# Expert visits over lists in halves of 64 rows: rows stationary instead of weights, fewer visits, a shorter slot table

## The chip, the cores and the metric

The kernel runs on one core of one Trainium2 chip. A core has TensorE (PE, matrix products into PSUM), VectorE (DVE), ScalarE (ACT), GpSimd (POOL) and SyncE (SP, which here only issues transfers), and 16 DMA engines that all queues share. The metric is device time in microseconds of one execution. All data is float32.

## The reference, cut to what matters

A vision transformer block on 32 images of 37 tokens (1184 tokens, 256 features): patch embedding, an attention with a gate and no softmax, and a mixture of experts. The change is in the last part:

```python
scores = sigmoid(x @ gate_weight.T)                 # 32 experts, 4 groups
# the best 2 groups, in them the best 6 experts: topidx, weights tw
g = einsum('th,ehi->tei', x, w_gate)                # hidden 128
u = einsum('th,ehi->tei', x, w_up)
eo = einsum('tei,eih->teh', silu(g) * u, w_down)
routed = einsum('te,teh->th', cw, eo)               # 6 experts of each token
lg = topidx[:, 0] // 2                              # one of 16 anchor experts, hidden 64
anchor = ...                                        # the same form, weight 0.1
out = routed + shared + 0.1 * anchor
```

So there are 48 lists of rows: 16 anchor lists with 1184 rows in all, 32 routed lists with 7104 rows in all. How long each list is, is known only when the routing has run.

## The kernel before, in words

**Front, 0 to some 178 us.** Embedding, attention and routing go through six blocks of tokens. For each block DVE computes which row of which list every token takes (`place`, its last instruction is L1245). POOL then scatters the token's row (256 features, the expert weights, the rows of the result) into the list in device memory (`rows_d`) with an indirect DMA per tile and choice, 77 in all (L457). The attention product (`attend`, L618) uses the array in four column strips of 32: 16 matmuls a tile, each strip with its own stationary and its own moving data, written to partitions 32r to 32r+31 of one PSUM bank. Every float32 matmul is two records in the trace, a transpose is one.

**The slot table.** The program is static, the lists are not. So the work is cut into a fixed number of visits of 128 slots, and a table tells for each visit where its rows start, which weights it uses, which column holds its weight and which sum it adds to. DVE computes it from the list lengths in 84 instructions (L1441 to L1524), PE turns the columns into rows (`table_rows`, `slot_bounds`), and DVE copies them to where registers are loaded from (L1530).

**The visits.** There are XT = 112: 25 of kind A (anchors: short lists packed into shared tiles of 128), then 24 of kind F (128 full rows of one expert), 31 of kind X and 32 of kind M (remainders of lists, packed into shared tiles of 128, where one tile can be visited for two or more lists). For visit i

- SP loads a register from the table and issues one load of 128 rows (`load_rows`, L413; six buffers);
- PE turns the rows (two 128x128 transposes, `turn_rows`, L812); ACT or DVE copies them out (L985, L1580);
- ACT copies the up weights of the expert into a buffer (`copy_up`, L981), since a stationary operand can't take its address from a register here;
- PE multiplies with the weights stationary and the turned rows moving (`up`, L823: four matmuls of 128 columns, two for an anchor); the result has the hidden features on partitions;
- ACT takes the silu (L990), DVE the product (`hidden`, L1597), which is already turned as the down product needs it;
- PE multiplies down (`down`, L838: hidden stationary, 256 columns of weights moving, at an address from a register);
- for F, ACT weighs the result and POOL sends it; else DVE adds the weighted rows into the packed tile (`accumulate`, L1589), and POOL sends the tile when its last list has been added (L483, 66 sends in all).

PE's order is written out by hand: `up(i)`, `turn_rows(i + 2)`, `down(i - 1)`. Each engine works its own instructions in order; semaphores join them. POOL issues the sends behind all scatters. At the end SP waits for all sends, loads the seven partial results of every token from `sums_d` (L419), DVE adds them (L1626) and SP stores the output (L434).

Before all this, SP fills 128 rows of zeros ahead of the lists (two DMAs of 7728 KB, L378), and POOL zeroes the packed tiles (L449, L476, L480).

Of the kernel before, what the change touches and what calls it, by code (L numbers as in the profile page):

```python
# [24 lines left out]
P = 128  # L25
# [35 lines left out]
LIST_ROWS = TOKENS  # L61
DUMMY_ROW = P + LISTS * LIST_ROWS
# [7 lines left out]
ROWS_PACKED = -(-TOKENS * TOPK // P)  # L70
LAST_FILLED = TOKENS * TOPK % P
FULL = -(-(TOKENS * TOPK - EXPERTS * (P - 1)) // P)
MIXED = ROWS_PACKED - FULL
EXTRAS = EXPERTS - 1
ANCHOR_PACKED = -(-TOKENS // P)
ANCHOR_TILES = ANCHOR_PACKED + ANCHORS - 1
KINDS = "A" * ANCHOR_TILES + "FFX" * 12 + "XM" * 6 + "XMM" * 13
XT = len(KINDS)
INDEX = [KINDS[:i].count(k) for i, k in enumerate(KINDS)]
TILE_AXIS, EXTRA_AXIS = 1000, 2000  # L80
RING = D + 1
GB = 6
PL = 3 * EXPERTS + ANCHORS


def routed(i):
    return KINDS[i] != "A"


def summed(i):  # L90

    return KINDS[i] != "F"


def sums_before(i):
    return sum(summed(k) for k in range(i))


def copied_by_act(i):
    return KINDS[i] != "F"  # L100


def copies_before(i):
    return sum(copied_by_act(k) == copied_by_act(i) for k in range(i))


def number_of(i):

    return {"A": 0, "F": TILE_AXIS, "M": TILE_AXIS + FULL, "X": EXTRA_AXIS}[KINDS[i]] + INDEX[i]
# [4 lines left out]
TRI4 = 3 * LISTS  # L114
SMALL = TRI4 + 23
PIECES = [[(0, 4), (4, 8), (8, NT)]] * (CHOICES - 1) + [[(0, 4), (4, 7), (7, 9), (9, 10), (10, NT)]]
assert KINDS.count("F") == FULL and KINDS.count("M") == MIXED and KINDS.count("X") == EXTRAS
assert all(KINDS[:i].count("X") >= min(EXTRAS, INDEX[i] + 1) for i in range(XT) if KINDS[i] == "M")
assert FULL * D <= ANCHOR_COLS and XT <= P
LATE_PIECES = 10  # L120
BIG = 3.0e38


def build(nc, pt, wt, posr, brow, wqkv, wo, wg1, wg2, lnwb, gwt, gbias, sgu, sd, wx,
          ident_c, cmask_c, turn_c, parity_c, cs_c, before_c, small_c, out):
    with ExitStack() as ctx:
# [56 lines left out]
        def dense(*shape):  # L183
# [5 lines left out]
            if len(shape) == 2:  # L189
# [13 lines left out]
        until_scattered = cut[0]  # L203
        xrow = dense(NT, ROW)
        padrow = dense(ROW)
        mixed = spent[:, 0:MIXED * RING]
        mixed_rows = mixed.bitcast(I32)
# [5 lines left out]
        of_lists = small[:, 0:3 * LISTS].rearrange("p (q l) -> p q l", q=3)  # L213
        iota_a, base0, tri4 = small[:, LISTS:LISTS + ANCHORS], small[:, 2 * LISTS:3 * LISTS], small[:, TRI4:TRI4 + 16]
        pcol, number, of_number, tile_number, spare_row, last_tile, first_w = (small[:, TRI4 + 16 + q:TRI4 + 17 + q]
                                                                                  for q in range(7))
        ring = sb("ring", [P, ANCHOR_PACKED * RING])
        h = sb("h", [P, NT, D])
        ring_rows = ring[:, :].bitcast(I32)
# [1496 lines left out]
```

## Time and profile before

| what | value |
|---|---|
| runs, us | 420.84, 417.67, 415.27; median 417.67 |
| profiled execution: span, first to last instruction | 412.1 us; the page gives no other time of this execution |
| mean granted TensorE clock | 0.930 |
| busy: PE / DVE / ACT / POOL | 343.3 / 278.0 / 190.0 / 181.7 us |
| chain that ended last, largest shares | PE L823 20%, PE L838 10%, PE L514 6%, PE L812 5% |

The span is what the trace covers; what lies between it and the time of a run is launch and end. A busy share is an average over stages with different limits, so the stages are read one by one in the rows below. In a timeline, a row that ends in x8 stands for eight records in a row; its first number is when the first one started, and the start of the next row tells when the array was free again.

### The profile page before, as it was taken

What the parts mean: (1) busy time and instruction counts of PE and PEld (TensorE: products, weight loads), DVE (VectorE), ACT (ScalarE), POOL (GpSimd) and SP (SyncE); (2) the same over time, 40 slices, a digit from 0 to 9 for tenths busy, and PEclk for the clock granted to TensorE, in tenths of its full rate; (3) what the DMA queues carried; (4) which work ended last, traced back from release to release, by engine and by line L of the source; (5) the groups of instructions that cost most, each with busy time, mean ns of one, the idle gap of its engine ahead of it and who ended that gap; (6) DMA issues with size and microseconds to landing.
All of it is one profiled execution on the core that took longest, in us unless ns stands there. A gap on an engine that the chain in (4) does not pass through costs nothing.

```text
span 412.1 us, 8817 instructions
## 1 busy us (share of the span) xinstructions
PE 343.3 (83%) x2552; PEld 299.1 (73%) x2552; DVE 278.0 (67%) x1171; ACT 190.0 (46%) x471; POOL 181.7 (44%) x159
## 2 busy tenths in 40 slices
PE   5999999999899968773889999999999999994000
PEld 3786978779687857561677789999999999993000
DVE  0466789989798886798357775555565665666675
ACT  1152153441545233400157777777877777771000
POOL 6000000588888768767871374344422344433000
PEclk9999999999999997985989999999999999998555
DMA  7999999986698643694555576555555559531998
GB/s 234 298 335 335 329 341 328 420 320 119 123 337 252 126 96 86 218 387 137 152 162 130 167 214 180 162 158 165 165 145 162 166 155 291 168 113 58 303 303 245
DMA packets 55823, 88.44 MB, mean 215 GB/s; under 512 B 16145, under 2 KB 46521, under 8 KB 55513
## 3 DMA queue, kind: packets, MB, share of 16 engines
q1 hardware_dynamic: 38192, 67.66, 52.9%
q0 software_dynamic: 16720, 19.48, 17.8%
q10 hardware_dynamic: 864, 0.73, 0.6%
q8 instruction: 21, 0.34, 0.3%
q14 instruction: 26, 0.21, 0.2%
HBM read 50.62 MB, written 37.09 MB: 213 GB/s over the span
## 4 chain that ended last, share of the span: by engine, by line
PE 60%; DVE 20%; DMA 8%; issue 3%; ACT 3%; SPq 3%; DVEq 2%; POOLq 0%
PE B L823 20%; PE B L838 10%; PE B L514 6%; PE B L812 5%; DMA W<-sums_d 4%; PE B L549 4%; PE B L632 3%; PE B L598 2%; PE B L618 2%; DVEq L319 2%; DMA e_sb<-rows_d 2%; SPq L419 2%; DVE ring L1589 1%; PE B L656 1%; DMA W<-in_pt 1%
## 5 line engine op out<-in xcount | busy, mean ns | idle before, releaser
L457 POOL DMA_INDIRECT rows_d<-spent,slot x77 | 104.1, 1352 | 97.3 <-issue 90.9
L823 PEld LDWEIGHTS B<-e_sb,UPW 128*128 128x128 f32 x796 | 105.4, 193 | 10.7 <-issue 5.5
L823 PE MATMUL B<-e_sb,UPW 128*128 128x128 f32 x796 | 108.9, 278 | 1.5 <-issue 1.5
L1597 DVE TENSOR_TENSOR e_sb<-e_sb,B 128x128 f32<-128x128 f32 (+1 forms) x112 | 32.3, 288 | 62.2 <-ACT e_sb L990 55.8
L981 ACT COPY UPW<-W 128x512 f32 (+1 forms) x112 | 63.9, 570 | 22.2 <-issue 13.9
L838 PE MATMUL B<-W,e_sb 128*128 x224 | 69.3, 391 | 0.8 <-DVE e_sb L1597 0.8
L483 POOL DMA_INDIRECT sums_d<-spent x32 | 31.1, 972 | 48.7 <-DVE spent L1589 47.9
L812 PE MATMUL B<-ident,e_sb 128*128 128x128 f32 x224 | 43.1, 274 | 1.9 <-DMA e_sb<-rows_d 1.8
L990 ACT ACTIVATE e_sb<-B 128x128 f32<-128x128 f32 (+1 forms) x112 | 30.9, 276 | 22.2 <-PE B L823 20.8
L514 PE MATMUL B<-W 128*111 128x256 f32 (+1 forms) x132 | 34.2, 406 | 4.6 <-DMA W<-in_pt 4.5
L483 POOL DMA_INDIRECT sums_d<-W,tok_full x24 | 23.2, 966 | 30.3 <-ACT W L995 29.7
L838 PEld LDWEIGHTS B<-W,e_sb 128*128 128x128 f32 x224 | 34.0, 192 | 3.5 <-issue 1.7
L985 ACT COPY e_sb<-B 128x256 f32<-128x256 f32 x88 | 32.3, 367 | 4.6 <-PE B L812 4.6
L514 PEld LDWEIGHTS B<-W 128*111 128x111 f32 (+1 forms) x132 | 23.3, 184 | 12.2 <-DMA W<-in_pt 5.3
L1589 DVE SCALAR_TENSOR_TENSOR spent<-B,wcol,spent 128x256 f32<-128x256 f32 (+1 forms) x63 | 30.4, 482 | 1.7 <-DVE spent L1574 0.8
L812 PEld LDWEIGHTS B<-ident,e_sb 128*128 128x128 f32 x224 | 28.5, 144 | 2.3 <-DMA e_sb<-rows_d 2.1
L1626 DVE TENSOR_TENSOR h<-h,W 112x1024 f32<-112x1024 f32 (+3 forms) x23 | 23.2, 1047 | 8.4 <-DMA W<-sums_d 8.4
L1289 DVE TENSOR_TENSOR e_sb<-B,spent 111x444 f32<-111x444 f32 (+1 forms) x44 | 23.6, 597 | 4.1 <-PE B L598 4.1
L1566 DVE TENSOR_TENSOR wcol<-e_sb,turn 128x1 f32<-128x1 f32 x112 | 17.2, 153 | 4.0 <-PE B L812 3.8
L598 PE MATMUL B<-W 32*111 32x222 f32 (+1 forms) x176 | 15.5, 369 | 4.8 <-ACT W L909 4.8
L549 PE MATMUL B<-W 128*128 128x222 f32 (+1 forms) x96 | 18.1, 341 | 0.6 <-ACT W L886 0.6
L606 PE MATMUL B<-spent 128*128 128x256 f32 x70 | 18.6, 414 | 0.0
(250 smaller groups left out, 524.0 us busy)
## 6 DMA issues: line engine op xcount, KB each, us to landing
e_sb<-rows_d SPq DMA_DIRECT2D x112, 161.0 KB, 2.3
rows_d<-spent SPq DMA_DIRECT2D x2, 7728.0 KB, 44.4
W<-in_wx SPq DMA_DIRECT2D x1, 6643.0 KB
W<-sums_d SPq DMA_DIRECT2D x13, 448.0 KB, 9.4
W<-in_wx SPq DMA_DIRECT2D x10, 516.5 KB, 9.5
W<-in_wx SPq DMA_DIRECT2D x1, 4576.0 KB, 18.7
W<-in_pt SPq DMA_DIRECT2D x4, 666.0 KB, 6.9
W<-sums_d SPq DMA_DIRECT2D x7, 336.0 KB, 11.1
```

What stands on the lines that cost most here:

```text
L457: pool.indirect_dma_start(rows_d, bass.IndirectOffsetOnAxis(ap=slot[0:n, t, j:j + 1], axis=0), xrow[0:n, t, :], None).then_inc(done, 16)
L483: pool.indirect_dma_start(sums_d, bass.IndirectOffsetOnAxis(ap=rows, axis=0), src, None).then_inc(done, 16)
L514: m = pe.matmul(B[0][0:TILES[t], i * D:(i + 1) * D], patch_view(b)[:, c, at:at + TILES[t]], w_patch[:, c, :], start=c == 0, stop=c == PC - 1)
L549: m = pe.matmul(B[4 + half][:, c * BT:c * BT + n], w_qkv[:, k, lo:lo + P], xnT[:, k, 0:n], start=k == 0, stop=k == KC - 1)
L812: m = pe.transpose(B[i % 2][:, k * P:(k + 1) * P], G[:, i % GB, k * P:(k + 1) * P], ident[:, :])
L823: mm = pe.matmul(B[2 + i % 2][:, m * P:(m + 1) * P], UPW[:, i % 2, at:at + P], GT[:, i % 2, k, :], start=k == 0, stop=k == KC - 1)
L838: pe.matmul(B[6 + i % 2][:, 0:D], hid[:, i % 2, :], weights, start=True, stop=True).then_inc(D_ps, 1)
L981: act.copy(UPW[:, i % 2, 0:n], W[:, bass.ds(e, size)][:, 0:n]).then_inc(upw_ok, 1)
L985: act.copy(GT[:, i % 2, :, :].rearrange("p k s -> p (k s)"), B[i % 2][:, 0:D]).then_inc(gt_by[True], 1)
L990: act.activation(S[0:n, i % 2, :], B[2 + i % 2][0:n, 0:P], ACT.Silu).then_inc(silu_ok, 1)
L1589: dve.scalar_tensor_tensor(sums, B[6 + i % 2][:, 0:D], wcol[:, i:i + 1], sums, ALU.mult, ALU.add).then_inc(acc_ok, 1)
L1597: dve.tensor_tensor(out[0:n, i % 2, :], S[0:n, i % 2, :], ups, ALU.mult).then_inc(H_ok, 1)
```

## The change

The lists are cut into halves of 64 rows. Each list has its tail of up to 64 rows, and the tails have fixed places: one visit of kind A for each anchor list and one of kind M for each expert, in whose second half (slots 64 to 127) the last 64 rows of that list stand. The weights of a second half are thus known when the program is built; the first half of such a visit takes a full half of any list, at an address from the table. What is left of full rows goes in visits of kind F, 128 rows of one expert (39), and one of kind a. So XT = 88: 16 A, one a, 32 pairs M F, 7 F.

In a visit the rows are now the stationary operand and the weights move, read in place at an address from a register; the copy of the up weights is gone. The result has rows on partitions; so the row's weight is applied in the hidden product, the hidden rows have to be turned by one more transpose and copied, and the down product uses them as stationary rows. Nothing is added up in packed tiles: every visit's result is copied by ACT into a ring of seven buffers and sent by POOL (88 sends), slots without a row to spare rows. The column of a slot's weight is picked by comparing 66 row elements with a code, not by a register. The table needs 22 DVE instructions to its first column; PE loads the weight addresses of four visits at once, SP those of two. The zero fill is 64 rows ahead of each list.

Constants and order:

```diff
-KINDS = "A" * ANCHOR_TILES + "FFX" * 12 + "XM" * 6 + "XMM" * 13
+HALF = P // 2
+LIST_ROWS = TOKENS + HALF
+FULL_GROUPS = (TOKENS * TOPK - TOPK) // HALF
+FULL = -(-(FULL_GROUPS - EXPERTS) // 2)
+KINDS = "A" * ANCHORS + "a" + "MF" * EXPERTS + "F" * (FULL - EXPERTS)
+GB, YB = 8, 7
...
+def pieces(i):
+    return 2 if tailed(i) else 1
...
+def tail_weights(i):
+    return ANCHOR_COLS + INDEX[i] * WX if routed(i) else INDEX[i] * ANCHOR_WX
```

SP and POOL:

```diff
-            for half in range(2):
-                sp.dma_start(of_list[half * P:(half + 1) * P, :, :],
-                             padrow[:, :].unsqueeze(1).to_broadcast([P, LISTS, ROW])).then_inc(empty, 16)
+            sp.dma_start(of_list[0:HALF, :, :],
+                         padrow[0:HALF, :].unsqueeze(1).to_broadcast([HALF, LISTS, ROW])).then_inc(empty, 16)
...
-                row = entry(mybir.EngineType.SP, 1, i, DUMMY_ROW + P)
-                sp.dma_start(G[:, i % GB, :], rows_d[bass.ds(row, P), :]).then_inc(g_ld[i % GB], 16)
+                n = P // pieces(i)
+                for q in range(pieces(i)):
+                    sp.dma_start(G[q * n:(q + 1) * n, i % GB, :], rows_d[bass.ds(rows[q], n), :]).then_inc(g_ld[i % GB], 16)
...
-            pool.memset(spent[:, 0:until_scattered], 0.0).then_inc(mixed_zero, 1)
...
+            for i in range(XT):
+                pool.wait_ge(to_ok, i + 1)
+                pool.wait_ge(Y_ok, i + 1)
+                pool.indirect_dma_start(sums_d, bass.IndirectOffsetOnAxis(ap=to_row[:, i:i + 1], axis=0),
+                                        Y[:, i % YB, :], None).then_inc(sent[i % YB], 16)
```

PE:

```diff
-            stay_busy(12, 3, w_sgu)
+            stay_busy(8, 3, w_sgu)
             table_rows()
             shared_down(3)
-            slot_bounds()
             shared_up(5)
+            table_codes()
...
-            pe.wait_ge(valid_ok, 1)
-            pe.wait_ge(hs_ok, NB - 2)
+            pe.wait_ge(codes_ok, 1)
+            pe.wait_ge(hs_ok, NB)
...
+            def moved(i, q, lo, n):
+                if q == 1:
+                    return W[:, tail_weights(i) + lo:tail_weights(i) + lo + n]
+                size = WX if routed(i) else ANCHOR_WX
+                return W[:, bass.ds(offsets[i], size)][:, lo:lo + n]
...
             def up(i):
...
+                n = 2 * (HIDDEN if routed(i) else ANCHOR_HIDDEN)
+                rows = P // pieces(i)
+                for k in range(KC):
+                    for q in range(pieces(i)):
+                        own = slice(q * rows, (q + 1) * rows)
+                        m = pe.matmul(B[2 + i % 2][own, 0:n], GT[:, i % 2, k, own], moved(i, q, k * n, n),
+                                      start=k == 0, stop=k == KC - 1)
+                m.then_inc(U_ps, 1)
+            def turn_hidden(i):
                 pe.wait_ge(H_ok, i + 1)
+                pe.transpose(B[4 + i % 2][:, 0:P], H[:, i % 2, :], ident[:, :]).then_inc(HT_ps, 1)
+            def down(i):
+                pe.wait_ge(ht_ok, i + 1)
...
+                for q in range(pieces(i)):
+                    own = slice(q * rows, (q + 1) * rows)
+                    m = pe.matmul(B[6 + i % 2][own, 0:D], HT[:, i % 2, own], moved(i, q, lo, D), start=True, stop=True)
+                m.then_inc(D_ps, 1)
...
+            for i in range(XT + 2):
+                if i % PER_LOAD == PER_LOAD - 1 and i + 1 < XT:
+                    load_offsets(i + 1)
+                if i < XT:
+                    up(i)
+                if i >= 2:
+                    down(i - 2)
                 if i + 2 < XT:
                     turn_rows(i + 2)
+                if 1 <= i <= XT:
+                    turn_hidden(i - 1)
```

ACT and DVE:

```diff
-            def copy_up(i):
...
+            def keep_result(i):
                 act.wait_ge(D_ps, i + 1)
+                if i >= YB:
+                    act.wait_ge(sent[i % YB], sent_until(i % YB, i))
+                act.copy(Y[:, i % YB, :], B[6 + i % 2][:, 0:D]).then_inc(Y_ok, 1)
+            def turned_hidden(i):
+                act.wait_ge(HT_ps, i + 1)
...
+                act.copy(HT[:, i % 2, :], B[4 + i % 2][:, 0:P]).then_inc(ht_ok, 1)
+            for i in range(XT + 2):
+                if i < XT:
+                    hidden_silu(i)
+                if i >= 2:
+                    keep_result(i - 2)
+                if 1 <= i <= XT:
+                    turned_hidden(i - 1)
...
+            def pick_columns(i):
+                dve.wait_ge(T_ps, i + 1)
+                dve.scalar_tensor_tensor(picked[:, i % 2, :, :], pick.unsqueeze(1).to_broadcast([P, 2, PICK]), code_of[:, i:i + 1],
+                                         G[:, i % GB, D:ROW].rearrange("p (q e) -> p q e", q=2),
+                                         ALU.is_equal, ALU.mult).then_inc(pick_ok, 1)
+            def sum_columns(i):
+                dve.reduce_sum(meta[:, i, :], picked[:, i % 2, :, :], axis=AX.X).then_inc(meta_ok, 1)
+            def result_rows(i):
+                dve.tensor_tensor(to_row[:, i:i + 1], meta[:, i, 1:2], spare[:, i:i + 1], ALU.add).then_inc(to_ok, 1)
             def hidden(i):
...
+                dve.scalar_tensor_tensor(H[:, i % 2, 0:n], B[2 + i % 2][:, n:2 * n], meta[:, i, 0:1], S[:, i % 2, 0:n],
+                                         ALU.mult, ALU.mult).then_inc(H_ok, 1)
+            for i in range(-2, XT):
+                if i >= 0:
+                    hidden(i)
                 if i + 2 < XT:
+                    pick_columns(i + 2)
+                    turned_copy(i + 2)
+                    sum_columns(i + 2)
+                    result_rows(i + 2)
```

## Rows read from the trace of the kernel before

**Rows 1.** Stages: stretch and its length, then busy us and instructions of each engine.
```profile
core 0: us, PE busy (x) PEld busy (x) DVE busy (x) ACT busy (x) POOL busy (x), PEclk, DMA share, GB/s
178.80:192.60 13.80, 5.49 (x23) 4.39 (x22) 12.81 (x85) 0.00 (x0) 11.05 (x9) 0.75 0.80 272
...
206.50:240.50 34.00, 32.06 (x193) 25.18 (x193) 24.50 (x96) 22.73 (x73) 15.57 (x11) 0.95 0.57 159
240.50:374.00 133.50, 133.50 (x1039) 129.09 (x1039) 78.11 (x348) 102.23 (x259) 55.09 (x58) 1.00 0.57 168
```

**Rows 2.** Timeline of PE in one routed visit: start, length, line, operation, count.
```profile
281.62 0.38 PE L812 MATMUL B<-ident,e_sb 128*128 128x128 f32 x2
281.84 0.60 PE L838 MATMUL B<-W,e_sb 128*128 x2
282.27 1.05 PE L823 MATMUL B<-e_sb,UPW 128*128 128x128 f32 x8
283.16 0.38 PE L812 MATMUL B<-ident,e_sb 128*128 128x128 f32 x2
```

**Rows 3.** Timeline of PE, the up part of two anchor visits in a row.
```profile
226.04 0.65 PE L823 MATMUL B<-e_sb,UPW 128*128 128x128 f32 x4
...
227.32 0.65 PE L823 MATMUL B<-e_sb,UPW 128*128 128x128 f32 x4
```

**Rows 4.** Timeline of PE, attention products in column strips around four transposes.
```profile
36.45 0.98 PE L618 MATMUL B<-e_sb,W 111*32 111x111 f32 x32
37.35 0.60 PE L539 MATMUL B<-ident,W 111*128 111x111 f32 x4
37.88 0.98 PE L618 MATMUL B<-e_sb,W 111*32 111x111 f32 x32
```

**Rows 5.** Timeline of DVE: the last slots, and the end of the table.
```profile
178.63 0.17 DVE L1245 SCALAR_TENSOR_TENSOR slot<-top_slots,ones 111x8 int32<-111x8 f32 x1
...
192.37 0.17 DVE L1524 TENSOR_TENSOR tcol<-tcol 128x1 f32<-128x1 f32 x1
```

**Rows 6.** Timeline of PE: the first rows of the first visit are turned.
```profile
203.14 0.41 PE L812 MATMUL B<-ident,e_sb 128*128 128x128 f32 x2
```

**Rows 7.** SP's row loads: the first six in the timeline; all 112, by line.
```profile
196.85 8.29 SPq L413 DMA_DIRECT2D e_sb<-rows_d  x6
...
DMA to landing us min/median/max: 2.2/2.3/6.2
```

**Rows 8.** POOL's scatters: first of the last tile, last of all; landing of all 77.
```profile
179.11 1.35 POOL L457 DMA_INDIRECT rows_d<-spent,slot  x1 [2.69 <-DVE slot L1245]
...
207.24 1.35 POOL L457 DMA_INDIRECT rows_d<-spent,slot  x1 [0.31 <-issue]
...
DMA to landing us min/median/max: 4.9/8.3/17.8
```

**Rows 9.** POOL's sends: two in a row in the timeline; landing of all 66.
```profile
234.13 0.97 POOL L483 DMA_INDIRECT sums_d<-ring  x1 [0.30 <-DVE ring L1589]
235.41 0.97 POOL L483 DMA_INDIRECT sums_d<-ring  x1 [0.30 <-DVE ring L1589]
...
DMA to landing us min/median/max: 2.4/2.4/4.5
```

**Rows 10.** Groups by line: busy, mean ns; then one instruction of the table, in the timeline.
```profile
L1597 DVE TENSOR_TENSOR e_sb<-e_sb,B 128x128 f32<-128x128 f32 (+1 forms) x112 | 32.3, 288 | 62.2 <-ACT e_sb L990 55.8
L985 ACT COPY e_sb<-B 128x256 f32<-128x256 f32 x88 | 32.3, 367 | 4.6 <-PE B L812 4.6
L1566 DVE TENSOR_TENSOR wcol<-e_sb,turn 128x1 f32<-128x1 f32 x112 | 17.2, 153 | 4.0 <-PE B L812 3.8
L1580 DVE COPY e_sb<-B 128x256 f32<-128x256 f32 x23 | 9.6, 415 | 0.0
187.62 0.33 DVE L1499 SCALAR_TENSOR_TENSOR e_sb<-e_sb,small 128x112 f32<-128x112 f32 x1
```

**Rows 11.** Register loads of SP: ns min/median/max, first and last start.
```profile
L319 SPq TENSOR_LOAD <-scratch x112: 262/268/1447, 195.3 to 363.0; - x112
```

More of the change, by code:

```diff
@@ L212, in build @@
         small = sb("small", [P, SMALL])
[L213 to L217, printed above, removed]
+        (base0, less, carry, cap, list_facts, iota_a, tri4, number, rows_before, from_end, spare_rows,
+         pick) = (small[:, column(name)] for name in COLUMNS)
+        pick_codes = list_facts[:, LISTS:2 * LISTS]
         h = sb("h", [P, NT, D])
-        ring_rows = ring[:, :].bitcast(I32)
         token_row = sb("token_row", [P, 2, NT], I32)
         to_rows = sb("to_rows", [P, NT])
-        spare = sb("spare", [P, 2])
         e_sb = sb("e_sb", [P, 2 * HEADS * TT])
@@ L315, in build, with entries, sent_until @@
         block = ctx.enter_context(nc.Block())
-        def entry(engine, q, i, top):
-            return nc.values_load(table[0:1, q, bass.ds(i, 1)], engines=(engine,), min_val=0, max_val=top,
-                                  skip_runtime_bounds_check_because="the table is computed within these bounds")
+        def entries(engine, of_tiles, top):
+            _, values = nc.values_load_multi_w_load_instructions(
+                of_tiles, engines=(engine,), min_val=0, max_val=top,
+                skip_runtime_bounds_check_because="the table is computed within these bounds")
+            return values
+        def sent_until(k, n):
+            return 16 * len(range(k, n, YB))
         def patch_view(b):
@@ L1413, in _ @@
             place(NB - 1)
-            E = EXPERTS
-            took = [0]
-            def tab(n):
-                v = tabs[:, took[0]:took[0] + n]
-                took[0] += n
-                assert took[0] <= tabs.shape[1]
-                return v
-            starts, ends, total, of_tile, mine = tab(PL), tab(PL), tab(E), tab(E), tab(PL)
-            facts = tab(4 * PL).rearrange("p (q l) -> p q l", q=4)
-            offset, many, shifted, slot_tile = (facts[:, q, :] for q in range(4))
-            held, begin, end, full, lead, behind = tab(LISTS), tab(LISTS), tab(LISTS), tab(E), tab(LISTS), tab(LISTS)
@@ L1428, in _ @@
-            new, away, some, rounded, over, span, own = (tab(LISTS), tab(LISTS), tab(LISTS), tab(E), tab(E), tab(ANCHORS),
-                                                         tab(LISTS))
-            picked = tab(3 * LISTS).rearrange("p (q l) -> p q l", q=3)
-            R, M, X, A = (slice(q * E, q * E + (E if q < 3 else ANCHORS)) for q in range(4))
-            LR, LA = slice(0, E), slice(E, LISTS)
-            ones_of = ones[:, 0:E]
-            def pack(q):
-                return tcol[:, q:q + 1]
```

485 lines of the change are left out of this document (169 added, 316 removed).

## The prediction

> **What bounds the kernel now.** I read the time by stages first. From 240.50 to 374.00 us, the 87 routed visits, TensorE is busy 133.50 of 133.50 us, while DVE has 78.11, ACT 102.23 and POOL 55.09 [rows 1]. That stage is TensorE's alone, so a visit's price is what its records take start to start. The anchor stage before it (206.50 to 240.50) has PE 32.06 of 34.00, yet its visits pace at 1.28 us, 226.04 to 227.32 [rows 3], where their records alone need 0.22 + 0.43 + 4 x 0.111 = 1.09 [rows 2]: there the loop of small steps around PE counts too. Between the routing and the first visit lies the table, 13.80 us with DVE busy 12.81 and PE 5.49 [rows 1].
>
> Second view: TensorE's records inside one routed visit [rows 2]. Two 128-column transposes take 281.62 to 281.84, 0.11 us each; the down matmul, two records of 256 columns, 281.84 to 282.27, 0.215 each; the up part, eight records of 128 columns, 282.27 to 283.16, 0.111 each. Time goes by moved columns, about 0.84 ns per column and record; every matmul is two records, a transpose one. The weight loads hide behind this.
>
> **The main edit: rows stationary, weights moving.** A visit of 128 rows of one expert (F) then has up = 2 matmuls of 256 columns = 4 x 0.215 = 0.86 us, down 0.43, and three transposes instead of two, since the hidden rows must be turned as well: 0.33. Sum **1.62 us**, against 1.54 now (281.62 to 283.16). Per visit this is no gain; the gain is in the number of visits, 88 for 112: 39 F, 32 M, 16 A, one a.
>
> **M and A carry two halves of 64 rows with different weights**, twice as many matmuls, each with 64 stationary columns and its own half of the output partitions. Whether the two halves run side by side decides everything. The kernel has such a case: the attention product (L618), with four column strips of 32. Its 32 records of 111 columns start at 36.45 and the next work starts at 37.35 [rows 4]: 0.90 us, where one after another they would need 32 x 0.093 (111 columns at 0.84 ns) = 2.98. So at least 3.3 of 4 strips overlap, each with its own moving data. I take two halves as fully overlapped. What the tiling costs is its change: 36.45 to 37.88 holds eight waves of L618, four transposes and two changes of tiling; 1.43 - 12 x 0.093 = 0.31 us for two changes. A tailed visit changes twice (into halves before up, out before the transposes). So
>
> - M: 0.86 + 0.43 + 0.33 + 0.31 = **1.93 us**
> - A: up 4 waves x 0.111 = 0.44, + 0.43 + 0.33 + 0.31 = **1.51 us**; a: 1.20 us.
>
> Routed: 39 x 1.62 + 32 x 1.93 = 125.0 us for 133.5, **gain 8.5**. Anchors: now 37.4 us from the first turn at 203.14 [rows 6] to 240.50, of which 25 x 1.28 = 32.0 are pace and 5.4 entry. After: 5.4 + 16 x 1.51 + 1.2 = 30.8, **gain 6.6**. Bounds: changes of tiling cost between nothing (48 x 0.31 = 15 us better) and double (15 worse); half tiles with an address from a register appear in no row.
>
> The Trainium skill speaks against full overlap: "TensorE: Matmul & The Clock Gate", section "Measured speedup vs the span model", has three column tiles at 2.38 times, an estimated 1.6 for two. By it the sum would be some 14 us worse. Our row shows 3.3 of 4 with a change of tiling inside, so the trace agrees with the page only in that a part is lost, and I price that part as the change.
>
> **The table.** 84 DVE instructions, L1441 to L1524, run from 178.83 (right behind L1245 at 178.63) to 192.37 [rows 1, 5], 0.16 us each. The new chain has 22 to its first column, 13 of them waited for: 3.6 us at that mean, 5.5 at 0.25 each, so the column is there at about 184.4, 8 us sooner. The rest then follows as before (10.7 us to the first turn at 203.14), but with other waits. SP issues its first row load at 196.85 [rows 7]; it will still wait for the last tile's anchor scatter, issued at 179.11, which lands after 8.3 us in the median, 17.8 at most [rows 8]. That gives 187.4, a register load of up to 1.4 [rows 11] and a landing of 6.2 [rows 7]: first rows at about 195.5. PE now also waits for all shared adds (hs_ok NB) and for the codes; these shared products and sums already lie inside the 10.7 us, so they keep PE until 195.1 at worst. **Gain 7**, bounds 0 (scatter lands at its latest) to 8.
>
> **What must hide.**
> - *Scatters and sends on POOL.* The last 18 scatters run from 179.11 until 208.59, 1.65 us each, set by the last slots at 178.63; the smaller zero fill frees the first scatter but cannot move this end. All sends queue behind it. ACT's keep_result(7) waits for send 0 (ring of 7), and behind it stand the copy of turned hidden rows and the next silu. Send 0 lands at about 208.6 + 1.0 + 2.4 = 212 [rows 9]; visit 7's result falls at about 195.5 + 5.4 + 9 x 1.5 = 214. Hidden by 2 us. After that POOL needs 1.28 per send (234.13 to 235.41), under every visit but a.
> - *DVE.* Hidden product 0.29, turned copy 0.42, one-column product 0.15 [rows 10]; the picking over 66 elements and its reduction lie between that 0.15 and the 0.33 of the 112-element form, taken 0.25 each. Sum 1.36 by durations, 1.6 with the waits between them: just under F. The register loads leave DVE.
> - *ACT.* Three passes, none above the 0.37 of the 128x256 copy [rows 10]: under 1.1. The weight copies go, but ACT was not the bound.
> - *SP.* M and F together: one register load, 0.27 us (1.4 while scatters run) [rows 11], three row loads of about 0.45 issue; 1.6 us against 3.55. A pair of A visits during scatters: 1.4 + 4 x 0.45 = 3.2 against 3.0, about even, with eight buffers ahead.
> - *PE's register load*, one for four visits instead of one each: no price, PE is gapless with the present ones.
> - Zeroing of packed tiles, fewer row bytes: off the path, nothing.
>
> **Tail.** The same send and reads follow the last down product. Before it stand one more transpose, 0.11 [rows 2], and a copy, 0.37 at most [rows 10], with their hops between engines: **+0.7** (bounds 0.5 and 1).
>
> **Sum.** 8.5 + 6.6 + 7 - 0.7 = 21.4. On the profiled execution: span 412.1 to 390.7. The page gives no time beyond the span; the median of the runs, 417.67, lies 5.6 above, kept: 417.67 - 21.4 = **396 us**.
>
> **The rivals.**
> 1. *The halves do not overlap* (the half whose weights come by register is held on the full array, say): slower than before. Place: up and down of M and A. Price: 32 x (0.86 + 0.43) + 16 x (0.44 + 0.43) = 55 us, time 451. It decides below an overlap r where 55 x (2/r - 1) = 21.4, r = 1.44. For it: every register address in the trace is on a full array. Against: 3.3 of 4 in L618. 0.12.
> 2. *They overlap in part.* Read the 0.90 us as lost overlap, 3.3 of 4 or 0.83 each, and let that come on top of the change: 2 x 0.83 = 1.65, 55 x (2/1.65 - 1) = 12 us, time 408. For it: the strips in our row have another width. 0.10. By the page of the Trainium skill named above it would be 410.
> 3. *Another engine becomes the bound*: DVE's chain, or hidden rows coming late to the turn (PE, copy, down in one visit), at 2.0 us a routed visit: 71 x 2.0 = 142 for 125, time 413. Against: DVE 1.6. 0.07.
> 4. *The table's gain doesn't come* (bound 0, the last anchor scatter landing late): 403. For it: landings up to 17.8. 0.10.
> 5. *The change of tiling costs nothing*, the 0.31 being waits: 381. Against: the records themselves leave 1.12 of the 1.43 us. 0.06.
>
> Forecast 0.55, own range 387 to 402.
>
> **Numbers.** 380 to 411 takes in the forecast, rivals 4 and 5 and most of rival 2: 0.55 + 0.10 + 0.06 + 0.08 = 0.79. 2% of 417.67, about what can be told from no change, is 8.4: faster below 409.3. Faster: forecast, 4, 5 and parts of 2 and 3, 0.71 + 0.05 + 0.02 = 0.78; same: the rest of 2 and 3, 0.10; slower: rival 1, 0.12.
>
> **What would show it.** F visits at 1.6 us and M at 1.9 in TensorE's timeline; in M, pairs of up records starting within some 10 ns, the next pair 0.215 later (0.215 between all records is rival 1); a gap of about 0.15 at each change of tiling; the first turn near 196; PE without idle time from the first M on. Wrong would be: PE waiting on DVE's product or ACT's copy in most visits (rival 3), or the first turn still at 203.

## The result, and the profile after

The changed kernel took **404.37 us** in the median of four executions (403.39 to 404.89), the kernel before 417.65 on the same chip (415.27 to 420.84): ratio **0.966, 95% interval 0.961 to 0.972**, 13.3 us faster. 396 us was forecast; 404.37 lies in the range of 380 to 411. In all that follows, a median takes only executions within 1.5% of the fastest of their kernel, since slower ones count as disturbed.

One correction comes first, as every stage is compared through it. The profiled execution of after took 404.71 us with a span of 402.9, so 1.8 us lie around the span, not 5.6. If as much lay around the span of before (412.1), its profiled execution was one of 413.9 us, 3.8 under the median.

The stages of after: the table, the anchors (first turn to first routed up), the routed visits (to the end of the last up); columns as in [rows 1].

```profile
184.46:189.32 4.86, 3.73 (x11) 2.68 (x9) 4.41 (x23) 0.00 (x0) 3.98 (x3) 0.70 1.04 398
201.23:235.11 33.88, 29.10 (x249) 17.20 (x247) 21.23 (x90) 13.38 (x47) 24.19 (x22) 0.90 0.64 180
235.11:359.45 124.34, 124.34 (x828) 89.13 (x828) 88.33 (x350) 62.68 (x212) 67.69 (x71) 1.00 0.58 174
```

The table is 4.9 us for 13.8, the routed stage 124.3 for 133.5 with PE busy throughout; in the anchors PE is busy 29.1 of 33.9 us only. SP's last wait ahead of the first row load:

```profile
SPq L332 <- DMA rows_d<-spent,slot: 2.6, 1, 2.6
```

It is the wait for a scatter of the last tile, as forecast: SP's first register load starts at 193.24 us, 9.0 behind the last slot (forecast 8.8).

Now PE's timeline through a mixed and a full visit:

```profile
281.24 1.08 PE L838 MATMUL B<-W,e_sb 128*64 x8
282.16 0.60 PE L856 MATMUL B<-W,e_sb 128*64 x4
282.69 0.44 PE L824 MATMUL B<-ident,G 128*128 128x128 f32 x2
282.97 0.27 PE L845 MATMUL B<-ident,e_sb 128*128 128x128 f32 x1
283.07 1.03 PE L838 MATMUL B<-W,e_sb 128*128 x4
283.94 0.59 PE L856 MATMUL B<-W,e_sb 128*128 x2
284.37 0.38 PE L824 MATMUL B<-ident,G 128*128 128x128 f32 x2
284.59 0.27 PE L845 MATMUL B<-ident,e_sb 128*128 128x128 f32 x1
284.79 0.44 PE L838 MATMUL B<-W,e_sb 128*64 x2
```

Start to start, the eight half records of the mixed up take 0.92 us (281.24 to 282.16), the four whole ones 0.87 (283.07 to 283.94): the halves seem to run side by side (experiment 1 asks whether they do). M and F together take 3.55 us (281.24 to 284.79), as forecast (1.93 + 1.62).

Then three lines on the start of the anchors: SP's register loads and row loads (190 to 236 us), ns as minimum/median/maximum, and what PE waited for, in us, times, longest.

```profile
L332 SPq TENSOR_LOAD <-row_table x12: 296/626/1184, 193.2 to 234.4; - x12
L430 SPq DMA_DIRECT2D G<-rows_d x43: 342/469/2146, 194.2 to 235.7; - x43
PE B L824 <- DMA G<-rows_d: 4.1, 5, 1.5
```

The first six register loads, up to 216.3 us, took 0.70 to 1.18 us, the six behind them 0.30 to 0.55. POOL's last scatter starts at 212.9 us, and a scatter lands 4.5 us after its issue at the least.

And the end: the last three sends, VectorE's first adds beside them, and the traffic of the late reads (372 to 391 us).

```profile
361.05 1.07 POOL L498 DMA_INDIRECT sums_d<-e_sb,to_row  x1 [0.45 <-issue]
362.46 1.66 POOL L498 DMA_INDIRECT sums_d<-e_sb,to_row  x1 [0.34 <-issue]
364.43 0.97 POOL L498 DMA_INDIRECT sums_d<-e_sb,to_row  x1 [0.30 <-issue]
...
360.06 3.22 DVE L1525 TENSOR_TENSOR h<-h,W 112x1024 f32<-112x1024 f32 x3
...
DMA packets 1540, 5.06 MB, mean 266 GB/s; under 512 B 193, under 2 KB 193, under 8 KB 1540
```

**The account of the two profiled executions**, 412.1 to 402.9, in us:

| stretch | before | after | forecast | came |
|---|---|---|---|---|
| start to last slot | 178.63 | 184.26 | 0 | +5.6 |
| last slot to first turn | 24.51 | 16.97 | -7 | -7.5 |
| first turn to first routed up | 37.4 | 33.9 | -6.6 | -3.5 |
| to the end of the last up | 133.6 | 124.3 | -8.5 | -9.3 |
| to the first late read | 5.8 | 8.0 | +0.7 | +2.2 |
| late reads to the end | 32.1 | 35.5 | 0 | +3.3 |

Two stages came as forecast. The four others are what experiments 3, 4 and 5 ask about.

### The profile page after: what moved, and what is told of

Read it like the earlier page. It is cut to its first block, busy times and chain, and to the rows that moved or that the text cites. A ratio compares the mean times of both kernels' runs of the same rounds, so it can differ in the third digit from the quotient of the medians.

```text
span 402.9 us, 7999 instructions
## 1 busy us (share of the span) xinstructions
PE 334.5 (83%) x2376; PEld 253.5 (63%) x2376; DVE 275.7 (68%) x1105; ACT 140.9 (35%) x399; POOL 195.0 (48%) x178
## 4 chain that ended last, share of the span: by engine, by line
PE 60%; DVE 14%; DMA 10%; SPq 7%; issue 4%; ACT 3%; POOL 1%; POOLq 0%; DVEq 0%
PE B L838 17%; PE B L856 8%; PE B L514 7%; PE B L824 6%; DMA W<-sums_d 5%; PE B L549 4%; SPq L430 4%; PE B L632 3%; PE B L598 2%; DMA rows_d<-spent,slot 2%; PE B L618 2%; PE B L845 2%; SPq L436 2%; POOL sums_d L498 1%; PE B L656 1%
## 5 line engine op out<-in xcount | busy, mean ns | idle before, releaser
L498 POOL DMA_INDIRECT sums_d<-e_sb,to_row x88 | 85.7, 974 | 65.4 <-ACT e_sb L1010 51.1
L838 PE MATMUL B<-W,e_sb 128*64 (+3 forms) x544 | 87.0, 368 | 0.7 <-DVE e_sb L1495 0.7
L838 PEld LDWEIGHTS B<-W,e_sb 128*64 128x64 f32 (+1 forms) x544 | 50.1, 155 | 15.9 <-issue 9.2
L856 PE MATMUL B<-W,e_sb 128*64 (+2 forms) x272 | 54.0, 389 | 1.2 <-ACT e_sb L1016 1.2
L1510 DVE SCALAR_TENSOR_TENSOR e_sb<-B,meta,e_sb 128x128 f32<-128x128 f32 (+1 forms) x88 | 29.8, 338 | 31.5 <-ACT e_sb L1004 31.0
L824 PE MATMUL B<-ident,G 128*128 128x128 f32 x176 | 37.2, 294 | 4.1 <-DMA G<-rows_d 4.1
L1010 ACT COPY e_sb<-B 128x256 f32<-128x256 f32 x88 | 32.8, 373 | 17.4 <-PE B L856 15.5
L824 PEld LDWEIGHTS B<-ident,G 128*128 128x128 f32 x176 | 21.0, 143 | 27.7 <-issue 16.9
L1495 DVE COPY e_sb<-B 128x256 f32<-128x256 f32 x88 | 36.8, 418 | 0.0
L1488 DVE SCALAR_TENSOR_TENSOR e_sb<-small,code_of,G 128x66 f32<-128x66 f32 x88 | 25.4, 288 | 15.6 <-PE B L824 11.3
L856 PEld LDWEIGHTS B<-W,e_sb 128*64 128x64 f32 (+1 forms) x272 | 27.7, 153 | 10.2 <-issue 2.4
L1016 ACT COPY e_sb<-B 128x128 f32<-128x128 f32 x88 | 23.4, 266 | 8.2 <-PE B L845 3.9
L845 PE MATMUL B<-ident,e_sb 128*128 128x128 f32 x88 | 24.3, 276 | 0.0
## 6 DMA issues: line engine op xcount, KB each, us to landing
rows_d<-spent SPq DMA_DIRECT2D x1, 3864.0 KB, 24.6
```

Of the source, the lines that this page charges most:

```text
L498: pool.indirect_dma_start(sums_d, bass.IndirectOffsetOnAxis(ap=to_row[:, i:i + 1], axis=0), Y[:, i % YB, :], None).then_inc(sent[i % YB], 16)
L824: m = pe.transpose(B[i % 2][:, k * P:(k + 1) * P], G[:, i % GB, k * P:(k + 1) * P], ident[:, :])
L838: m = pe.matmul(B[2 + i % 2][own, 0:n], GT[:, i % 2, k, own], moved(i, q, k * n, n), start=k == 0, stop=k == KC - 1)
L845: pe.transpose(B[4 + i % 2][:, 0:P], H[:, i % 2, :], ident[:, :]).then_inc(HT_ps, 1)
L856: m = pe.matmul(B[6 + i % 2][own, 0:D], HT[:, i % 2, own], moved(i, q, lo, D), start=True, stop=True)
L1010: act.copy(Y[:, i % YB, :], B[6 + i % 2][:, 0:D]).then_inc(Y_ok, 1)
```

## The experiments

**1. Do the halves need to be issued in turn?**

```diff
-                for k in range(KC):
-                    for q in range(pieces(i)):
+                for q in range(pieces(i)):
+                    for k in range(KC):
```

> The changed kernel with the two loops of up exchanged: all four matmuls of one half, then all four of the other, instead of the two halves in turn. Theory, side by side: the eight matmuls of a half-tiled up take 0.92 us where the four of a whole one take 0.87 us because neighbours that go to different halves of the array run at the same time; in this order only the pair in the middle has such a neighbour, so an up of a mixed visit takes about 1.6 us and one of an anchor visit about 0.4 us more than now: 32 x 0.7 + 16 x 0.4 = 29 us, about 433 us. Rival, half price: a matmul with 64 stationary columns simply takes half as long as one with 128; then the order is free and the time stays within 2 us of 404.4.

404.91 us (402.66 to 407.42; ratio to before 0.966, 0.956 to 0.976): nothing changed. PE's timeline of one mixed up, cut off at 283.24, then at 283.26, then whole, with the down behind it:

```profile
282.98 0.44 PE L838 MATMUL B<-W,e_sb 128*64 x2
...
282.98 0.66 PE L838 MATMUL B<-W,e_sb 128*64 x4
...
282.98 1.09 PE L838 MATMUL B<-W,e_sb 128*64 x8
283.89 0.61 PE L856 MATMUL B<-W,e_sb 128*64 x4
```

Up to 283.24 two records have begun, 0.02 us later four. At half the price one after another they would be spaced 0.11 us and a third would have begun by 283.20. So "half price" falls too, though the time agrees with it: the records still start in twos, one with weights at a register's address (first half) and one with fixed weights (second half), although the kernel has all of one half first (two matmuls, four records). The halves start as if each had a queue of its own; what orders them so isn't shown. What I had expected, that only neighbours in the program overlap, was wrong; that two run side by side was right.

**2. What does a mixed visit pay?** TensorE treats M visits as whole ones; the tail's own weights are left out.

```diff
+def halves(i):
+    return 1 if KINDS[i] == "M" else pieces(i)
...
-                    for q in range(pieces(i)):
+                    for q in range(halves(i)):
```

> The changed kernel with the 32 mixed visits computed as whole ones on TensorE (both halves with the weights of the full half; the tail half's own weights are left out); loads, picks and sends are as they were. Theory, as in the prediction: the mixed visit costs 0.31 us more than a full one through its two changes of tiling and nothing else; the pair takes 2 x 1.62 = 3.24 us instead of 3.55 us, and the time falls by 32 x 0.31 = 9.9 us to about 394.5. Rival, the second load or the pick is what costs: the pair stays at 3.55 us, the time at 404.4. Rival, another engine is next: the pair stops between, at 3.3 to 3.5 us.

396.48 us (0.946, 0.937 to 0.955), 8.4 under the kernel of experiment 1 on the same chip. Two visits that were M and F:

```profile
280.76 1.03 PE L842 MATMUL B<-W,e_sb 128*128 x4
...
282.38 1.03 PE L842 MATMUL B<-W,e_sb 128*128 x4
...
284.01 0.81 PE L842 MATMUL B<-W,e_sb 128*128 x3
```

280.76 to 284.01 is 3.25 us for 3.55, as expected; the routed stage is 9.5 us shorter (114.86). The second load and the pick cost nothing here. **Next, the same visits in another order**, M before F:

```diff
-KINDS = "A" * ANCHORS + "a" + "MF" * EXPERTS + "F" * (FULL - EXPERTS)
+KINDS = "A" * ANCHORS + "a" + "M" * EXPERTS + "F" * FULL
```

> The changed kernel with the order of the routed visits changed from mixed and full in turn to all 32 mixed ones and then all 39 full ones; nothing else. Theory, as in the prediction: a mixed visit pays 0.31 us for two changes of tiling, from whole turns to halves and back, and does so whoever its neighbour is; 32 mixed at 1.93 us and 39 full at 1.62 us take the same 125 us, the time stays within 1 us of 404.4. Rival, it is the alternation of kinds that costs: the mixed ones go at about 1.7 us and the time falls by 5 us or more. Rival, SP: two row loads and half a register load for every visit in a row, 1.4 to 1.6 us by this trace, don't keep up with 32 mixed visits; the time rises.

406.72 us (0.967, 0.959 to 0.974); M at 1.92, F at 1.62 us, the stage 124.7. One mixed visit and the next up:

```profile
259.64 1.08 PE L838 MATMUL B<-W,e_sb 128*64 x8
260.56 0.60 PE L856 MATMUL B<-W,e_sb 128*64 x4
261.09 0.44 PE L824 MATMUL B<-ident,G 128*128 128x128 f32 x2
261.37 0.27 PE L845 MATMUL B<-ident,e_sb 128*128 128x128 f32 x1
261.57 1.08 PE L838 MATMUL B<-W,e_sb 128*64 x8
```

The down's four records need 2 x 0.215 = 0.43 and take 0.53; the two turns behind them need 0.22 and take 0.28; the third turn needs 0.11 and takes 0.20; the up needs 0.87 and takes 0.92. The four excesses make 0.30, all at the two places where tiling changes. **Taking the changes away**, in the same order, by turning in halves too:

```diff
+            def turned(j, dst, src):
+                if not (0 <= j < XT and tailed(j)):
+                    return pe.transpose(dst, src, ident[:, :])
+                for lo in (0, HALF):
+                    m = pe.matmul(dst[lo:lo + HALF, :], src[:, lo:lo + HALF], ident[:, :], start=True, stop=True)
+                return m
```

> The same order, and in the anchor visits with tails and the mixed visits the three turns are two half matmuls each against the identity, instead of whole transposes, so that TensorE stays in halves from the first mixed visit to the last. Theory, the change of tiling is what costs 0.155 us each: the mixed visit falls from 1.93 to 1.62 to 1.65 us (32 x 0.3 = 9.5 us), the later anchor visits from 1.57 us to between 1.26 and 1.45 us (SP's two issues and half a register load take about 1.45), 1 to 2.5 us in the nine that SP is ahead of; the time falls by 10.5 to 12 us to about 393. Rival, the halves themselves cost (twice as many weight loads): the visits stay at 1.93 and 1.57 us, the time at 404. Rival, VectorE or SP is next: the mixed visit stops at 1.7 to 1.8 us, the time at 397 to 400.

405.44 us (405.08 to 405.71; 0.966, 0.957 to 0.974): no gain, M at 1.95, late anchors at 1.75.

```profile
259.77 1.03 PE L845 MATMUL B<-W,e_sb 128*64 x8
260.63 0.60 PE L863 MATMUL B<-W,e_sb 128*64 x4
261.06 0.61 PE L824 MATMUL B<-ident,G 128*64 128x128 f32 x8
261.50 0.39 PE L824 MATMUL B<-ident,e_sb 128*64 128x128 f32 x4
261.72 0.82 PE L845 MATMUL B<-W,e_sb 128*64 x6
```

The gaps are gone: the up takes 0.86, the down 0.43, as much as whole ones take (0.87, 0.43), so without a change of tiling the overlap is complete. But a transpose is one record per turn, a float32 matmul two, so the three turns take 0.66 (261.06 to 261.72) where whole transposes take 0.33. What was saved is paid again; none of the three theories had that. **Halving the number of changes instead**, two visits per round:

```diff
+            for i in range(0, XT + 1, 2):
+                for j in (i + 2, i + 3):
+                    if j < XT:
+                        turn_rows(j)
+                for j in (i - 2, i - 1):
+                    if j >= 0:
+                        turn_hidden(j)
+                for j in (i, i + 1):
+                    if j < XT:
+                        up(j)
...
+                for j in (i - 2, i - 1):
+                    if j >= 0:
+                        down(j)
```

> The order of all mixed visits ahead of all full ones again, and the visits worked off two at a time on TensorE, ScalarE and VectorE: the whole transposes of two visits (four turns of rows, two of the hidden part), then the two ups and the two downs in halves, so that a pair of mixed visits has two changes of tiling instead of four; the arithmetic is that of the changed kernel. Theory, the change costs 0.155 us each: a mixed visit goes from 1.92 to 1.77 us (32 x 0.15 = 5.0 us), a late anchor visit from 1.57 to 1.42 to 1.45 us (1 us in all, SP's issues stand in the way), a full one stays at 1.62 us; the time falls by 5 to 6 us, to 399 to 401. Rival, the longer way round: in a round of two, a turned copy or a hidden part comes too late for TensorE, it waits 0.15 us or more per visit, and the time stays at 404 or rises, the full visits above 1.62 us with it.

```profile
260.47 1.95 PE L840 MATMUL B<-W,e_sb 128*64 x16
262.25 1.03 PE L858 MATMUL B<-W,e_sb 128*64 x8
263.21 0.66 PE L826 MATMUL B<-ident,G 128*128 128x128 f32 x4
263.70 0.38 PE L847 MATMUL B<-ident,e_sb 128*128 128x128 f32 x2
264.01 0.44 PE L840 MATMUL B<-W,e_sb 128*64 x2
...
PE B L826 <- DMA G<-rows_d: 10.4, 8, 2.5
```

260.47 to 264.01: 1.77 us a mixed visit, as expected; full ones stay at 1.62, late anchor pairs take 2.69 where they wait for nothing. So a change costs 0.15 us, twice confirmed, and the routed stage is 120.3 us for 124.3. The time did not show it: 403.31 us in the median of four (399.85 to 405.79; 0.965, 0.959 to 0.972), level with the changed kernel. In the profiled execution (401.57 us) 10.4 us went to waits for row loads at the start of the anchors, and the first late read came 9.3 us after the last up instead of 8.0. No version here beats the changed kernel beyond doubt.

**3. Why did the anchors gain half?** First, half of the first loads from ScalarE's queue:

```diff
-                for q in range(pieces(i)):
+                for q in range(pieces(i) if i >= GB else 1):
...
+            for i in range(GB):
+                act.dma_start(G[HALF:P, i, :], rows_d[bass.ds(first[2 * i + 1], HALF), :]).then_inc(g_ld[i], 16)
```

> The changed kernel with the tail halves of the first eight visits loaded from ScalarE's queue (which is idle from 195 to 204 us) instead of SP's. Theory, SP's issuing bounds the start of the anchor stage: 16 loads and 4 register loads took SP from 193.2 to 211.3 us, so the row loads of visits 2 to 8 came late; with half of them elsewhere the first eight visits are loaded by about 204 us, the stage from first turn to first routed up falls from 33.95 to 30.5 to 31.5 us, and the time by 2.5 to 3.5 us to about 401.5. Rival, the landing is what is late (the 33 scatters still under way until 214 us): the stage stays over 33 us and the time within 1 us of 404.4.

400.77 us (399.4 to 404.06; 0.956, 0.948 to 0.964), but the profiled execution has 34.62 us for the stage: the first six visits went faster (10.5 us for 14.3), then three took 3.8, 1.9 and 2.7 us, the first with a wait of 2.1 us for its rows, the others with the clock granted at 0.78 and 0.52. Issues were slow on ScalarE's queue as well:

```profile
L1023 ACTq DMA_DIRECT2D G<-rows_d x8: 559/858/1705, 192.9 to 200.0; - x8
L332 SPq TENSOR_LOAD <-row_table x14: 294/300/1905, 191.1 to 235.8; - x14
```

So it isn't SP's number of issues alone. Next SP waits until every scatter has landed:

```diff
             sp.wait_ge(table_ok, 1)
+            sp.wait_ge(scat, 16 * NT * TOPK)
```

> The changed kernel with SP waiting for all scatters to land before its first row load, so that nothing else is issued while the anchors start. Theory, the scatters make SP's issues slow (register loads of 0.7 to 1.2 us and loads of up to 2.1 us each while POOL scatters, 0.3 and 0.47 us later): without them the visits go at 1.57 us almost from the first, and first turn to first routed up takes 30 to 31 us instead of 34 to 38 us; the first turn itself moves to about 220 us and the time to about 418. Rival, two issues per visit are too many for SP in any case: the stage stays at 33 us or more, the time about 421.

One execution, 420.04 us; the stage takes **29.70 us** (220.82 to 250.52), with visits at about 1.57 us from the fourth on, at the same two issues a visit. Register loads and row loads in the stage:

```profile
L332 SPq TENSOR_LOAD <-row_table x12: 295/298/506, 217.0 to 250.1; - x12
L431 SPq DMA_DIRECT2D G<-rows_d x42: 293/468/1217, 217.7 to 250.7; - x42
```

Register loads take 0.30 us in the median for 0.63 and nowhere above 0.51; a row load still took 1.22 once. The first sixteen row loads with their four register loads take SP 13.3 us instead of 18.0, and from the start of its issue to its last packet one of them takes 1.9 us in the median instead of 3.6. The granted clock of the stage is the same (0.89 for 0.90), so it isn't the clock; within the stage PE waits under 1 us for rows, in the changed kernel 4.1. So **the cause is that the rows are loaded while POOL scatters**: register loads then take 0.7 to 1.2 us and row loads up to 2.15. How much of it is issue and how much landing is not separated, as both go with the scatters. Loading by both queues and with one register load for eight visits did not help in the version with turns in halves:

> The kernel of the turns in halves, and the first eight visits' rows loaded by SP and ScalarE side by side as in the experiment on ScalarE's queue, SP with one register load for the eight instead of four. Theory, while the scatters run each register load and each issue costs 0.5 to 2 us whoever issues it, so what helps is fewer of them in a row: SP issues 8 loads and 1 register load instead of 16 and 4, and the anchor stage is 1.5 to 3 us shorter than without; about 391. Rival, the scatters take back what is gained, as they did when ScalarE alone was added (the wait moved from visits 2 to 6 to visits 7 to 9): within 1 us of the kernel without it.

407.39 us (405.15 to 409.29; 0.970, 0.960 to 0.980) against 405.44 without; the stage is 33.8 for 38.5 us, but the execution spent it elsewhere (first turn 19.2 us behind the last slot, late reads 4.67 us a part for 3.96). Whether such loads gain anything in time is not settled.

**4. Why is the tail longer?** The late parts come at 4.71 us each instead of 4.13 (starts of their adds, five parts). I tried the place of sums_d, its length in the kernel before, and its length in the changed one.

```diff
-        rows_d = nc.dram_tensor("rows_d", [HALF + LISTS * LIST_ROWS, ROW], F32).ap()
+        rows_d = nc.dram_tensor("rows_d", [HALF + LISTS * LIST_ROWS + 320, ROW], F32).ap()
```

> The changed kernel with 320 unused rows of 1288 bytes added to rows_d, so that all that is placed behind it (sums_d) stands at the same remainder of 4096 bytes as in the kernel before (3072, where the change made it 512). Theory, place: the six late parts are read at 4.74 us each instead of 4.13 us because sums_d was moved off multiples of 1024 bytes; here the pace goes back to 4.1 to 4.2 us a part, the 4096-byte packets from 236 to about 194 ns, and the time falls by 3 to 4 us, from 404.4 to about 401. Rival, size or traffic: the pace hangs on the larger sums_d or on where the results were written; the part stays at 4.7 us and the time within 1 us of 404.4.

```diff
-        sums_d = nc.dram_tensor("sums_d", [SPARE_ROW + P, D], F32).ap()
+        sums_d = nc.dram_tensor("sums_d", [SPARE_ROW + P * XT, D], F32).ap()
```

> The kernel before with one edit of the change alone: sums_d made as long as in the changed kernel (8632 + 128 x 112 rows instead of 8632 + 128). Theory, length of sums_d: the late parts are read at 4.6 to 4.8 us each instead of 4.13 us, and the time rises by 6 x 0.6 = 3.6 us over the kernel before. Rival, something else of the changed kernel: the parts stay at 4.1 to 4.2 us and the time within 1 us. Beside that, its front is the front of the kernel before in a second execution: if the change costs nothing ahead of the last slot, the last slot stands somewhere in 178 to 185 us by the clock that was granted; if it stands at 178 to 179 us again while all five profiles of kernels with the change show 182.0 to 185.0 us, the change does cost some 3 to 6 us there.

```diff
-        sums_d = nc.dram_tensor("sums_d", [SPARE_ROW + P * XT, D], F32).ap()
+        sums_d = nc.dram_tensor("sums_d", [SPARE_ROW + P * YB, D], F32).ap()
...
-    small[:, column("spare_rows")] = SPARE_ROW + row[:, None] + P * np.arange(XT)
+    small[:, column("spare_rows")] = SPARE_ROW + row[:, None] + P * (np.arange(XT) % YB)
```

> The changed kernel with the spare rows of sums_d shared by every seventh visit, so that sums_d has 8632 + 128 x 7 rows instead of 8632 + 128 x 88. Theory, length of sums_d: the late parts come at 4.1 to 4.2 us each instead of 4.74 us, the time falls by 3 to 4 us against the changed kernel, to about 401. Rival, something else: the parts stay at 4.7 to 4.8 us, the time within 1 us of 404.4.

With the place undone the profiled execution (408.74 us) has 4.79 us a part, which speaks against the place; a single execution enters the median, 401.94 us, and it has no profile, so the time can't tell. The longer sums_d in the kernel before: 4.35 us, 417.81 us, ratio 0.997 (0.993 to 1.002); the shorter one in the changed kernel: 4.52 us, 405.09 us (0.971, 0.965 to 0.977). In the kernel before, the length costs no time that can be told from none, where 3.6 us were expected; length falls as the cause. Two rows of traffic, of the experiment with short sums_d (373.9 to 391.9 us) and of the one with turns in halves (376.2 to 392), whose tail is the changed kernel's own:

```profile
DMA packets 1534, 5.04 MB, mean 280 GB/s; under 512 B 192, under 2 KB 192, under 8 KB 1534
```

```profile
DMA packets 1535, 5.04 MB, mean 319 GB/s; under 512 B 192, under 2 KB 192, under 8 KB 1535
```

Over all kernels with the change the pace ran from 3.96 to 4.92 us a part, against 4.13 and 4.35 in the two profiles of before's code; eleven of the twelve lie above both. Between two kernels with the same tail (3.96 and 4.71) it differs by more than the term to be explained; what sets it stays open.

The sends, held apart from VectorE's adds:

```diff
+            dve.wait_ge(Y_ok, XT)
             for c in range(CHOICES):
```

> The changed kernel with VectorE's first three adds of the result held back until the last down has been copied, so that they no longer run beside the last sends. Theory, VectorE's large adds slow the sends that POOL issues: the last but one send takes 0.97 us instead of 1.66, the first late part is asked for 0.7 us earlier after the last routed up, and the time falls by about 0.7 us, to 403.7. Rival, the send is long for a reason of its own: 1.66 us stays, and the time stays at 404.4. Rival, the adds are needed early: the first late add then starts later than its part has landed, and the time rises by up to 3 us.

```profile
365.33 0.97 POOL L498 DMA_INDIRECT sums_d<-e_sb,to_row  x1 [0.44 <-issue]
366.74 1.34 POOL L498 DMA_INDIRECT sums_d<-e_sb,to_row  x1 [0.44 <-issue]
```

The last but one send is back at 0.97 us, the last, now beside the adds, at 1.34 for 0.97. So the adds can slow a send (the one at 361.05, beside them too, took only 1.07), but the first late read came 7.8 us after the last up instead of 8.0; the time, 405.00 us (0.970, 0.964 to 0.976), shows nothing. The rest is the order at the end. The last down, before and after:

```profile
374.94 0.69 PE L838 MATMUL B<-W,e_sb 128*128 x2 [0.34 <-DVE e_sb L1597]
```

```profile
362.01 0.69 PE L856 MATMUL B<-W,e_sb 128*128 x2 [0.61 <-ACT e_sb L1016]
```

It starts 0.8 us behind the end of the last up before and 2.6 after, as each of the last two downs waits alone for the copy of its own turned hidden rows: 1.8 of the 2.2 us. From the landing of the last send to the first late read, SP's steps through the waits for seven buffers take 0.6 us, where one wait took 0.06: another 0.5.

**5. The front.** The kernel before in a second profile (experiment with the longer sums_d), its last slot:

```profile
180.36 0.17 DVE L1245 SCALAR_TENSOR_TENSOR slot<-top_slots,ones 111x8 int32<-111x8 f32 x1
```

178.63 and 180.36 us without the change; 181.50 to 185.03 in all twelve profiles with it. In eleven of those twelve TensorE's clock was granted at its lower level (0.5, 1.2 GHz) once or more between 14 and 150 us, in neither of the two before. Counted by the six blocks of tokens (from one block's last slot to the next) the trace tells where the time goes:

| block | 1 | 2 | 3 | 4 | 5 | 6 |
|---|---|---|---|---|---|---|
| before, us | 72.4 | 24.8 | 24.8 | 24.6 | 24.3 | 7.7 |
| changed, us | 75.1 | 26.4 | 24.8 | 24.4 | 25.8 | 7.8 |

Blocks 2 and 5 are those in which the clock was granted lower (0.94 for 1.00 and 0.74 for 0.86); ahead of the fall in block 2, at 88.4 us, PE had been busy 4.07 of 4.40 us. Over all fourteen profiles block 3 takes 24.8 us with the clock up throughout and 26.4 with one such stretch. So about half of the 5.6 us comes with the clock and half in the first block. Whether the change causes either (between 14 and 150 us its DMA share is 0.61 where before has 0.90) or two profiles are too few was not tried.

The second profile also moved the yardstick. Its anchors took 41.2 us with the code that took 37.4 in the first, its span 417.2. Means of the two, against means of five profiles of the changed kernel and of experiments 1 (halves in order), 2 (order of visits), 4 (short sums_d, late adds), whose work is the same:

| stretch | before, 2 | changed, 5 | difference |
|---|---|---|---|
| start to last slot | 179.5 | 183.8 | +4.3 |
| to the first turn | 23.8 | 17.4 | -6.5 |
| to the first routed up | 39.3 | 36.0 | -3.3 |
| to the end of the last up | 133.6 | 124.5 | -9.2 |
| to the first late read | 5.8 | 8.0 | +2.2 |
| to the end | 32.6 | 35.4 | +2.8 |

The sum is -9.7, 3.6 short of the 13.3 between the medians; single profiled executions differ by that much.

## Why the prediction was right, and where it missed

- **Right: the routed visits.** F 1.62 and M 1.93 us are what the trace has (1.62 and 1.92 apart, 3.55 as a pair); 9.3 us gained for 8.5. Rivals 1 and 2 fell with the 0.92 against 0.87 us and the starts in twos. By the page "TensorE: Matmul & The Clock Gate" of the Trainium skill, section "Measured speedup vs the span model", I had estimated 1.6 for two halves; the trace has 2 x 0.87 / 0.92 = 1.89 with the change of tiling in it, and with the turns in halves, where none is left, 0.86 us, which is full overlap.
- **Right: the price of the tiling change**, 0.31 us for two, read from eight waves of attention products and four transposes in [rows 4]: shown by taking the halves away (3.25), by the gaps in the grouped order (0.30) and by halving the number of changes (1.77). Rival 5 fell.
- **Right: the table.** 24.51 to 16.97 us, gain 7.5 for 7, first turn 17 us behind the last slot, through the wait that was forecast. The first turn itself stood at 201.2 us, not near 196, because the last slot came 5.6 us later. Rival 4 fell, though the time is near its 403: what is missing is missing elsewhere.
- **Wrong: the step on SP.** "A pair of A visits during scatters: 1.4 + 4 x 0.45 = 3.2 against 3.0, about even, with eight buffers ahead." I priced the register load above what it took under scatters (1.18 us at most) but the row loads at a calm value, and the changed kernel doubles those. They took up to 2.15 us each, and the first eight visits took SP 4.5 us a pair for 3.2 (without scatters 3.3), so the buffers were not ahead: the stage took 33.9 us in this profile and 36.0 in the mean for 30.8. Without scatters it takes 29.7; the visit itself (1.57 for 1.51) was nearly right.
- **Mis-sized: the tail.** +0.7 counted one transpose and one copy; it measured +2.2 in both accounts: +1.8 since each of the last two visits makes that round on its own, +0.5 for SP's seven waits. The pace of the late reads was not in the prediction at all and stays open.
- **Wrong: what a profile stands for.** The 5.6 us "around the span" were 1.8, and the rest, if so, was an execution quicker than its median. So the sum was made from an anchor stage of 37.4 us and a front of 178.6 us that a second profile shows at 41.2 and 180.4. The front, which I held fixed, moved by some 4 us to the bad, in part with the granted clock; whether the change does that stays open.
- Rival 3 did not occur: from the first routed up to the end of the last one PE was busy 124.34 of 124.34 us.

The direction came from work that is counted on one saturated engine and held to 1 us; the miss of 8 us is in the anchors and the tail, as experiments 3 and 4 show, and in the front and the pace of the late reads, whose causes stay open.

## What to carry to other kernels

A stage in which one engine is busy without a gap can be forecast from its records, start to start, to a per cent; price its neighbours, where transfers are issued while scatters run, by the slow values of every instruction issued there, not by medians. Two halves of the array with different weights are nearly free, but count the places where whole and half work alternate, at 0.15 us each, and put like work side by side within a round of instructions (grouping whole visits alone gained nothing). Take a second profile of the same code before explaining differences of a few us.

## What was not expected of the hardware

- Two halves of the array do not keep the program's order between them: four records for one half and then four for the other, in the kernel's order, started in pairs within 0.02 us. The page "TensorE: Matmul & The Clock Gate" of the Trainium skill, section "The mechanism", has matmuls as a strict first in, first out; across two column halves this trace differs.
- While POOL's indirect scatters run, register loads on SP take 0.70 to 1.18 us (0.30 in the median without), row loads up to 2.15 us (without, up to 1.22), on ScalarE's queue 0.86 in the median.
- An indirect send of 0.97 us on POOL took 1.07 to 1.66 us beside VectorE's adds of 112 x 1024 (four sends in three profiles).
- A turn by float32 matmuls against the identity, in halves, costs two records, a transpose one: 0.22 against 0.11 us.
